# Late diagonal blocks of two convolutions placed side by side in the TensorE array

## The reference

```python
def _L0_cond_ref(u, length, log_dt, C, log_A_real, A_imag, D):
    mask = (jnp.arange(Lq) < length[:, None]).astype(u.dtype)
    u_m = u * mask[:, None, :]
    kernel = _get_kernel(log_dt, C, log_A_real, A_imag, Lq)
    n = 2 * Lq
    k_f = jnp.fft.rfft(kernel, n=n)
    u_f = jnp.fft.rfft(u_m, n=n)
    y = jnp.fft.irfft(u_f * k_f, n=n)[..., :Lq]
    y = y + u_m * D[:, None]
    return y * mask[:, None, :]
...
x = x + _L0_attn_ref(_L0_cond_ref(x, itok_B_8_3872, ...), L0_attn_Wq, ...)
x = x + _L0_ffn_ref(_L0_cond2_ref(x, L0_cond2_weights, itok_B_0_15), ...)
```

## Time and profile before

| | us |
|---|---|
| median of 3 runs | 875.67 (875.13 to 877.23) |
| the profiled execution | 874.4 |
| its span, first to last instruction | 872.6 |
| TensorE busy in the span | 853.4 |
| convolutions 2 to 31 | 31.95 to 162.80 |

### The profile page before, as it was taken

How to read it: one execution, slowest core, us unless ns; L and a number is a source line. 1 busy time by engine, 2 the same in 40 slices (tenths; PEclk the granted TensorE clock), 3 DMA queues, 4 the chain that set the end, 5 groups by cost and what they waited for, 6 DMA issues and landing times.

```text
span 872.6 us, 24726 instructions
## 1 busy us (share of the span) xinstructions
PE 853.4 (98%) x10922; PEld 740.5 (85%) x10922; DVE 464.7 (53%) x898; ACT 221.4 (25%) x377; POOL 449.0 (51%) x346
## 2 busy tenths in 40 slices
PE   3999999999999999999999999999999999999998
PEld 2899999988888888887777777777779999999998
DVE  6556541122522222238887777888845755545444
ACT  4546543100000000023133223333334322211220
POOL 3344445502377555649968888887746422102220
PEclk9999999999999999999999999999999999999999
DMA  3777878514254322254634454546436211222211
GB/s 92 179 198 196 207 201 206 186 49 147 101 178 125 87 73 73 49 180 135 159 106 150 146 182 157 171 166 186 135 133 225 97 64 57 77 98 98 97 50 49
DMA packets 96907, 114.90 MB, mean 132 GB/s; under 512 B 44064, under 2 KB 66336, under 8 KB 96800
## 3 DMA queue, kind: packets, MB, share of 16 engines
q1 hardware_dynamic: 93808, 112.29, 42.9%
q10 hardware_dynamic: 2480, 0.51, 0.3%
q0 software_dynamic: 512, 0.53, 0.2%
HBM read 80.16 MB, written 33.13 MB: 130 GB/s over the span
## 4 chain that ended last, share of the span: by engine, by line
PE 96%; DMA 1%; DVE 1%; SPq 1%; issue 0%; ACT 0%
PE ps L988 25%; PE ps L1277 21%; PE ps L1599 15%; PE ps L652 10%; PE ps L1627 5%; PE ps L952 5%; PE ps L663 4%; PE ps L1233 3%; PE ps L1213 3%; PE ps L1509 2%; PE ps L1644 1%; PE ps L1643 1%; SPq L608 1%; DMA kpad<-ksb 1%; DMA toep<-kpad 0%; PE ps L1611 0%
## 5 line engine op out<-in xcount | busy, mean ns | idle before, releaser
L1599 PE MATMUL ps<-wb_hi,xf 128*128 128x424 f32 x440 | 127.0, 356 | 0.0
L988 PE MATMUL ps<-y_hi,w_hi 128*128 128x512 f32 x320 | 125.1, 391 | 0.0
L988 PE MATMUL ps<-y_hi,w_lo 128*128 128x512 f32 x320 | 124.5, 389 | 0.0
L988 PE MATMUL ps<-y_lo,w_hi 128*128 128x512 f32 x320 | 124.5, 389 | 0.0
L1575 POOL TENSOR_TENSOR xf<-xs,xf 128x512 fp32r<-128x512 f32 x32 | 42.1, 1345 | 124.8 <-DVE xs L1563 124.8
L1277 PE MATMUL ps<-y_hi 128*128 128x512 f32 x256 | 102.9, 402 | 0.0
L1277 PE MATMUL ps<-y_hi,y_lo 128*128 128x512 f32 x256 | 100.2, 391 | 0.0
L1277 PE MATMUL ps<-y_lo,y_hi 128*128 128x512 f32 x256 | 100.1, 391 | 0.0
L652 PE MATMUL ps<-xc,toep 64*128 64x192 f32 (+4 forms) x1088 | 96.8, 330 | 1.2 <-DMA toep<-kpad 1.2
L652 PEld LDWEIGHTS ps<-xc,toep 64*128 64x128 f32 x1088 | 90.2, 187 | 4.7 <-issue 1.6
L1599 PEld LDWEIGHTS ps<-wb_hi,xf 128*128 128x128 f32 x440 | 82.7, 188 | 2.3
(11 more groups left out here) (190 smaller groups left out, 1618.5 us busy)
## 6 DMA issues: line engine op xcount, KB each, us to landing
toep<-kpad SPq DMA_DIRECT2D x124, 136.0 KB, 3.7
xc<-in_dram SPq DMA_DIRECT2D x32, 256.0 KB, 4.2
q_rows<-rf SPq DMA_DIRECT2D x32, 256.0 KB, 2.6
q<-q_rows SPq DMA_DIRECT2D x16, 512.0 KB
xr<-in_dram SPq DMA_DIRECT2D x16, 512.0 KB, 4.5
x_scratch<-xr SPq DMA_DIRECT2D x16, 512.0 KB, 2.7
x<-x_scratch SPq DMA_DIRECT2D x16, 512.0 KB, 4.1
out_dram<-x SPq DMA_DIRECT2D x15, 512.0 KB, 2.8
```

What stands on the lines that cost most here:

```text
L988: mm = pe.matmul(kq_bank(n), w[a][:, j, :], yt[b][:, j, g * 512:(g + 1) * 512], start=(j == 0 and a + b == 0), stop=(j == NJ - 1 and a == 1))
L1599: mm = pe.matmul(dst[:, PLAIN:], xf(i, idx, a)[:, t, :], wb(c, idx, t), start=(start and t == 0 and a + c == 0), stop=(t == 3 and a == 1), ...
```

## The change

1. The Toeplitz strip is cut by its first 64 columns, those that hold the zeros: `toep` is L = 1024 columns wide, each DMA starts HALF = 64 elements later in `kpad`, and its pieces are 512 columns (in convolution 0: 256, 256, 512) instead of 544 (320, 256, 512). `rows_of` names columns by distance in half blocks.
2. The product (0,1) is taken out of `WIDE`, which leaves eight.
3. An even convolution has its late half of (0,1) as the last two matmuls, on the late half of the array's columns, in its own banks.
4. An odd convolution has its late half of (0,1) as its first two matmuls (`late_alone`), but on the early half of the columns. Their output is therefore partitions 0 to 63, and goes to PSUM of its own: columns 256 to 511 of banks 2((n + 1) mod 3) and the next, `near_late`.
5. ScalarE copies it from there to partitions 64 to 127 of `ym` (`take_late`, L793), issued after the activations of convolution n - 1.
6. VectorE's mask of an odd convolution becomes three instructions on 64 partitions each: the late half of PSUM is added to the copy (L744), the early half is masked (L745), the late half is masked in place (L747).
7. New waits: TensorE ahead of an odd convolution n > 1 for `v_mask` of n - 2 and ahead of an even n > 0 for `a_late` of n - 1; ScalarE for `pe_late` and `g_ylo` of n - 2; VectorE for `a_late`.

```diff
@@ toep and its loads @@
-        toep = sb("toep", [P, TR, L + HALF], F32, s1)
+        toep = sb("toep", [P, TR, L], F32, s1)
...
-        FIRST_ROWS = [(0, 2 * P + HALF), (2 * P + HALF, NJ // 2 * P + HALF), (NJ // 2 * P + HALF, L + HALF)]
-
-        ROW_HALVES = [(0, (L + HALF) // 2), ((L + HALF) // 2, L + HALF)]
+        FIRST_ROWS = [(0, 2 * P), (2 * P, NJ // 2 * P), (NJ // 2 * P, L)]
+
+        ROW_HALVES = [(0, L // 2), (L // 2, L)]
...
-                          bass.AP(kpad, head(n, r) * (KROW + 1) + lo, [[1, HALF], [1, hi - lo]])).then_inc(landed, 16)
+                          bass.AP(kpad, head(n, r) * (KROW + 1) + HALF + lo, [[1, HALF], [1, hi - lo]])).then_inc(landed, 16)
@@ the products @@
+        def near_late(n):
+
+            free = 2 * ((n + 1) % 3)
+            return ps[0:HALF, free:free + 2, NJ * NB:2 * NJ * NB]
+
+        def moving(n, c, d, r):
+
+            return xc[r * HALF:(r + 1) * HALF, n // XH % XR, 1 - c, n % XH, 0:(NJ - d) * NB]
+
+        def rows_of(n, r, dist, count):
+
+            return toep[r * HALF:(r + 1) * HALF, n % TR, dist * HALF:(dist + count) * HALF]
...
-        def narrow(pe, n, c, d, start, stop=False):
-
-            for half in range(2):
-                at = d * P + (1 + half - c) * HALF
-                for r in range(2):
-                    rows = slice(r * HALF, (r + 1) * HALF)
-                    mm = pe.matmul(ps[half * HALF:(half + 1) * HALF, 2 * (n % 3) + r, d * NB:NJ * NB], toep[rows, n % TR, at:at + HALF],
-                                   xc[rows, n // XH % XR, 1 - c, n % XH, 0:(NJ - d) * NB],
-                                   start=start, stop=stop)
+        def narrow(pe, n, c, d, half, start=False, stop=False):
+
+            for r in range(2):
+                mm = pe.matmul(ps[half * HALF:(half + 1) * HALF, 2 * (n % 3) + r, d * NB:NJ * NB], rows_of(n, r, 2 * d - c + half, 1),
+                               moving(n, c, d, r), start=start, stop=stop)
             return mm
 
-        TILES = [(d, c) for d in range(NJ) for c in range(2)]
-        WIDE, NARROW = TILES[:NJ + 1], TILES[NJ + 1:]
+        def late_alone(pe, n):
+
+            for r in range(2):
+                mm = pe.matmul(near_late(n)[:, r, :], rows_of(n, r, 0, 1), moving(n, 1, 0, r), start=True, stop=True)
+            mm.then_inc(pe_late, 1)
+
+        WIDE = [(d, c) for d in range(NJ // 2) for c in range(2) if d > 0 or c == 0] + [(NJ // 2, 0)]
+        NARROW = [(NJ // 2, 1)] + [(d, c) for d in range(NJ // 2 + 1, NJ) for c in range(2)]
@@ convolve @@
             if n % 2 == 0:
+                if n > 0:
+                    pe.wait_ge(a_late, n // 2)
...
                 for d, c in NARROW:
-                    mm = narrow(pe, n, c, d, start=False, stop=((d, c) == NARROW[-1]))
+                    for half in range(2):
+                        narrow(pe, n, c, d, half, stop=(half == 0 and (d, c) == NARROW[-1]))
+                mm = narrow(pe, n, 1, 0, 1, stop=True)
             else:
+                if n > 1:
+                    pe.wait_ge(v_mask, n - 1)
+                late_alone(pe, n)
                 for d, c in [WIDE[0]] + NARROW:
-                    mm = narrow(pe, n, c, d, start=((d, c) == WIDE[0]))
+                    for half in range(2):
+                        narrow(pe, n, c, d, half, start=((d, c) == WIDE[0]))
@@ VectorE @@
+        def mask(v, n):
+
+            pair = ps[:, 2 * (n % 3):2 * (n % 3) + 2, 0:NJ * NB]
+            kept = across(valid[:].rearrange("p j b -> p (j b)"), 2)
+            if n % 2 == 0:
+                return v.tensor_tensor(ym[:, 0, :, :], pair, kept, ALU.mult)
+            late, early = ym[HALF:P, 1, :, :], ym[0:HALF, 1, :, :]
+            v.wait_ge(a_late, (n + 1) // 2)
+            whole = v.tensor_tensor(late, pair[HALF:P, :, :], late, ALU.add)
+            v.tensor_tensor(early, pair[0:HALF, :, :], kept[0:HALF, :, :], ALU.mult)
+            chain(v, whole)
+            return v.tensor_tensor(late, late, kept[HALF:P, :, :], ALU.mult)
@@ ScalarE @@
+        def take_late(act, n):
+
+            act.wait_ge(pe_late, (n + 1) // 2)
+            if n > 1:
+                act.wait_ge(g_ylo, n - 1)
+            act.activation(ym[HALF:P, 1, :, :], near_late(n), ACT.Copy).then_inc(a_late, 1)
...
+                if n % 2 == 0:
+                    take_late(act, n + 1)
```

## The result

The changed kernel takes **877.58 us** (median of 22 runs, 875.26 to 880.3); the kernel before takes 875.99 beside it (22 runs, 874.05 to 877.88). The ratio is 1.0018, 95% interval 1.0011 to 1.0025: slower by 1.6 us, which is within the 0.3% of no change, and outside my range of 867.8 to 874.0.

What follows compares the result with a forecast made beforehand. TensorE, busy 98% of the span, was taken to bound the kernel. Its gain of -6.6 us, +0.5 at convolution 2 and +0.1 at convolution 4 gave -6.0, so 875.67 became 869.7 us, range 867.8 to 874.0.

Steps and rivals of the forecast that it cites:

- TensorE's term: Matmuls of the convolutions: a net gain of 0.44 us per pair, 15 of 16 pairs counting, 6.6 us.
- 8.0 us for a pair: Sign that the forecast is right: TensorE's matmuls repeat in 8.0 us per pair of convolutions, against 8.43 before.
- the rival: Even-to-odd border: waits let the late half in a pass late, half of 0.43 us lost per pair; 873.0 us, chance 0.10.
- Place 2: Every fourth convolution (4, 8, ...): the copy comes last in the longest VectorE and ScalarE row; slack 1.4 us, cost 0.
- evacuation is late: Rival at every fourth convolution: half-partition mask steps or copies cost double, 1.7 us lost in seven rounds; 881.6 us, chance 0.06.
- a gap released by ScalarE every fourth convolution: Sign that the forecast is wrong: TensorE idles every fourth convolution until ScalarE releases it.
- Place 1: Convolution 2: newly waits for the first ScalarE copy, queued behind four kernel stores; +0.5 us, ends +0.2 and +0.9.
- Place 3: `toep` loads, read at convolution 8: slack of 0.8 us shrinks by 0.44; cost 0, up to 0.3 in each of seven rounds.
- My rival: `toep` becomes the bound: 0.44 us lost in each of seven rounds, 3.0 us; 872.7 us, chance 0.05.
- Place 4: End of the convolutions: the three-step last mask takes 1.2 to 1.4 of 1.9 us before the next stage; cost 0.

Runs made afterwards that it cites:

- e15: e13 with GpSimd's exponents of a kernel group moved one convolution earlier: 870.28 us, ratio 0.992 against the kernel before.
- the control: The kernel before with only a third slot for the input columns and their loads issued behind the even strip: 875.57 us, ratio 0.9987.
- e6: The changed kernel with GpSimd's exponents of a kernel group moved one convolution earlier: 875.21 us, ratio 0.9985 against the kernel before.
- e4: The changed kernel with ScalarE's copy going to a buffer of its own and put ahead of the even convolution's activations: 872.44 us, ratio 0.9958.
- e5: e4 with the odd convolution's waits moved ahead of the even one's last late half: 872.75 us, ratio 0.995 against the kernel before.
- e13: e5 with a third slot for the input columns, loaded on SyncE behind the even convolution's strip, about four convolutions ahead: 870.49 us, ratio 0.9941.
- e11: e4 with four `toep` slots, the odd convolution's waits moved ahead of the border and GpSimd's exponents one convolution earlier: 873.49 us, ratio 0.9974.
- e8: e4 with each channel's Toeplitz strip loaded by one DMA of 256 KB instead of two of 128 KB: 875.67 us, ratio 0.9989.
- e2: The changed kernel with copy and its wait kept, but a one-instruction odd mask that leaves the odd late half out of the output: 872.76 us, 0.9968.
- e12: e5 with the input columns' loads issued from ScalarE's queue instead of SyncE's: 876.16 us, ratio 1.001 against the kernel before.

## Why the prediction was wrong, step by step

- **TensorE's term, 0.44 a pair, times 15: right in the price.** In e15 convolution 4 starts at 41.76 and the convolutions end at 157.17, 115.41 us; before, 41.40 to 162.80, 121.40. That is 5.99 us over 14 pairs, 0.43 each, and the 8.0 us for a pair that I named. The new order of loading has no part in it: the control takes 121.57 us from convolution 4 to the end. TensorE's busy time in e15 is 847.1 us, 6.3 less than before. In the changed kernel as it stands a pair takes 8.09: 0.34 gained. The late half does enter a little late; the rival had half of 0.43, the trace shows 0.09.
- **Place 2, "slack 1.4, cost 0": this is the step that failed.** The row of steps was the right one, and so were the masks and the copy. But I moved VectorE's steps later with the durations that they had before, when GpSimd stood idle beside them or had begun after them. They now start behind a GpSimd instruction and beside it: the phases with their exponents (84.11 to 88.97, 4.86 us, where 81.52 to 85.53, 4.01, was enough), L509 and L512 with y_lo (the tables take 91.11 to 94.50, 3.39 instead of the 2.15 that I carried over). Together 2.1 us; 1.4 of it was slack, so 0.7 would be late, and 0.93 to 0.99 is, in four rounds of the seven. e6 shows the first part by experiment, the second is read from the time lines. What it cost was the copy at the row's end: in e4 the steps are as long, and no wait for ScalarE is left. It is the rival "evacuation is late", by another hand: I priced it for halves of the partitions and gave it 0.06, and its sign, a gap released by ScalarE every fourth convolution, is what the trace shows.
- **Place 1, +0.5: the size was right (0.64), the rest wasn't.** I took no account of the clock: an idle stretch of 1.86 us instead of 1.16 in front of convolution 2, and in about half of the runs some 1.4 us on top.
- **Place 3, `toep`, cost 0: wrong, and hidden by the first error.** With the chain mended, TensorE waits some 2.4 us for strips behind convolution 2 (e4, and 2.5 in e5), where it had no wait before. I read the slack of 0.8 from one convolution and took off 0.44 once, but the loads are paced by TensorE's own progress, and the 1.3 us of input columns ahead of a strip is a fixed time that doesn't shrink; that this is the reason is my reading, for which e13 speaks. My rival had 3.0 us for it at 0.05.
- **Place 4, the end, cost 0: right.** The next stage begins without a gap.
- From convolution 4 to the end the changed kernel takes 166.17 - 42.95 = 123.22 us, 1.8 more than before. -0.34 x 14 = -4.8; waits for the copy 3.9 (5.7 less 1.86), for a strip 0.7; three borders and two wide runs that are longer by 0.2 to 0.4 each, 1.4. That makes +1.2; 0.6 us of it I can't place.

So the 6.0 us of the forecast is about what the change is worth (some 5.3 to 5.9 in e15 with the control taken off), but not what it gives without two covers: a place for the copy and an order of loading. VectorE's steps away from GpSimd's help the change as it stands (e6), but with the other two in place no gain by them can be told (e13 and e15). That the medians of e13 and e15, 870.5 and 870.3 us, lie so near the 869.7 forecast is in part luck: the order of loading, which wasn't in the sum, gives up to 1 us of it.

## What to carry to other kernels

A step of one engine keeps its measured duration only as long as what runs beside it is the same: when a change moves VectorE's work, look at what GpSimd does in the new place, and price steps with two SBUF inputs that start behind a GpSimd instruction at double or more (2.1 to 2.7 times here) before calling a slack sufficient. Or take the step that is wanted first out of the long row, as e4 does with the copy. When a faster TensorE is forecast, add up for every load that its progress releases the issues that stand ahead of it on the queue, not the landing alone. If mending one cover restores less than was lost, the next bound is already there: read the waits again.

## What the runs showed that I had not expected

- The granted clock after a gap isn't settled by the gap's length. After 1.86 us (the change), 1.94 (e6), 1.97 (e11) and 2.31 (e8) of idleness it was down to 0.50 and 32 wide records took 4.4 to 4.6 us; after 1.71 (e2), 1.64 (e13) and even 1.99 (e12, ahead of the records at 60.31, which took 2.87) it stayed at 1.00. e11's stretch behind its gap, in which the clock falls after some 0.8 us (0.61 is the mean), and e12's (same columns as above):

```profile
94.82:98.22 3.40, 3.40 (x24) 3.26 (x26) 0.91 (x4) 1.09 (x2) 1.76 (x2) 0.61 0.78 215
```

```profile
60.31:63.70 3.39, 3.39 (x56) 3.22 (x60) 0.99 (x4) 1.10 (x2) 1.95 (x3) 1.00 0.78 217
```

- VectorE's step on two SBUF inputs takes 0.75 us with GpSimd idle and 1.60 beside it for two instructions of 128x256, and one of them 0.42 to 0.43 and 1.03 to 1.14. The one that starts first is not the one that is slowed: L512 ahead of y_lo took 0.42 and y_lo 1.09.
- Two column halves of the array fed by different convolutions run at once without a price that I could find (8.00 us a pair), but a wait between them costs 0.09 us a pair. In the chains above it shows as the pieces of 0.09 and 0.13 us, which with the waits moved away are 0.23 and 0.20; in the time lines the two halves start 0.06 us apart (71.99 and 72.05 with the own buffer) and 0.01 without the waits (53.91 and 53.92). That they stay apart until the next wide block is inferred from the price, not shown.
